# A one-hot selector made and refilled by halves in a fused four-layer graph kernel

## The reference, cut to what matters

```
nd = adj_d > 0                                    # neighbours that are kept
vals = jnp.where(nd[..., None], x[:, None, :, :], jnp.inf)
s = jnp.sort(vals, axis=2)                        # over the neighbours
nv = nd.sum(2)
for tau, w in zip((0.25, 0.5, 0.75), (0.25, 0.5, 0.25)):
    pos = tau * max(nv - 1, 0)
    lo, hi, frac = floor(pos), ceil(pos), pos - floor(pos)
    v_lo, v_hi = s at lo, s at hi                 # per node and feature
    agg = agg + w * (v_lo + frac * (v_hi - v_lo))
out = x + agg
y = (relu(out @ W1 + b1) @ W2 + b2) * mask
```

## Time and profile before

| | |
|---|---|
| median of three runs | 3531.01 us |
| profiled execution, device time | 3535.06 us |
| its span in the trace | 3533.3 us |
| busy: PE, DVE, ACT | 2577.4 us (73%), 2814.0 us (80%), 2151.4 us (61%) |
| share of the chain that ended last: PE, DVE, ACT, transfers | 47%, 23%, 19%, 3% |
| mean granted TensorE clock | 0.838 of full |
| rounds with units | 650 to 3200 us |

### The profile page before, as it was taken

One profiled execution on the slowest core, in us unless ns is written; L12 is line 12 of the kernel. 1 busy time (PEld: TensorE's weight loads), 2 busy tenths in 40 slices (PEclk: granted clock), 3 DMA queues, 4 the chain that ended last, 5 costly groups with the idle time before them and its releaser, 6 DMA issues.

```text
span 3533.3 us, 48449 instructions
## 1 busy us (share of the span) xinstructions
PE 2577.4 (73%) x17770; PEld 1184.8 (34%) x17770; DVE 2814.0 (80%) x5341; ACT 2151.4 (61%) x3176; POOL 13.7 (0%) x24
## 2 busy tenths in 40 slices
PE   0000114788888888888888888888888888986996
PEld 0000002333333333333333333333433343333665
DVE  7999989877878778787878787878778787745676
ACT  2112433677777777777777767777777777752232
POOL 0000000000000000000000000000000000000000
PEclk6555557899998989899999999998989999987777
DMA  2002000001010101001010101010100101010011
GB/s 63 0 0 60 6 0 21 10 19 22 19 29 9 33 10 31 12 27 19 19 20 19 19 20 31 9 29 11 33 9 29 19 19 20 2 26 24 25 36 36
DMA packets 157564, 74.67 MB, mean 21 GB/s; under 512 B 125192, under 2 KB 140698, under 8 KB 157082
## 3 DMA queue, kind: packets, MB, share of 16 engines
q1 hardware_dynamic: 153210, 70.68, 8.7%
q10 hardware_dynamic: 4128, 1.05, 0.2%
HBM read 42.27 MB, written 16.83 MB: 17 GB/s over the span
## 4 chain that ended last, share of the span: by engine, by line
PE 47%; DVE 23%; ACT 19%; issue 8%; DMA 3%; SPq 0%; DVEq 0%; ACTq 0%
PE rows L621 12%; PE ring L584 8%; PE found_bank L631 6%; ACT hot L1043 6%; PE bcast L597 5%; ACT below L1008 3%; DVE keys L1306 2%; DVE keys L1305 2%; PE bcast L702 2%; PE bcast L711 2%; ACT prod L1036 2%; PE bank L873 2%; DVE delta L1347 1%; DVE delta L1345 1%; DVE perm L1349 1%
## 5 line engine op out<-in xcount | busy, mean ns | idle before, releaser
L1043 ACT ACTIVATE hot<-bcast,consts 128x1024 bf16<-128x1024 f32 x744 | 831.9, 1118 | 235.8 <-PE bcast L597 235.1
L621 PE MATMUL rows<-hot,table 128*64 128x512 bf16 x4608 | 696.9, 411 | 0.0
L584 PE MATMUL ring<-member,neigh_t 128*128 128x512 bf16 x2048 | 524.2, 400 | 46.8 <-ACT words L1000 28.7
L1036 ACT ACTIVATE prod<-rows 128x512 f32<-128x512 f32 x600 | 361.6, 603 | 119.6 <-PE rows L621 119.4
L631 PE MATMUL found_bank<-prod,consts 128*64 128x512 f32 x1536 | 416.5, 621 | 0.0
L597 PE MATMUL bcast<-idx_t,consts 32*128 32x512 f16 x1488 | 306.9, 409 | 105.7 <-ACT hot L1043 103.4
L610 PE MATMUL rows<-fine_rows,consts 32*128 32x512 bf16 x768 | 310.5, 404 | 85.3 <-DVE prod L1455 52.8
L521 PE MATMUL ring<-identb,adj_b 128*128 128x128 bf16 x256 | 35.1, 266 | 387.2 <-ACT adj_b L928 376.0
L584 PEld LDWEIGHTS ring<-member,neigh_t 128*128 128x128 bf16 x2048 | 186.6, 102 | 370.1 <-issue 111.1
L621 PEld LDWEIGHTS rows<-hot,table 128*64 128x64 bf16 x4608 | 213.9, 113 | 271.2 <-issue 203.0
L1455 DVE TENSOR_SCALAR prod<-rows 128x512 f32<-128x512 f32 x168 | 115.6, 689 | 176.9 <-PE rows L621 171.6
(11 more groups left out here) (348 smaller groups left out, 4581.1 us busy)
## 6 DMA issues: line engine op xcount, KB each, us to landing
late<-in_adj_dram SPq DMA_DIRECT2D x16, 1024.0 KB, 5.3
fine_rows<-fine_t SPq DMA_DIRECT2D x512, 24.0 KB
adjt_d<-neigh_t SPq DMA_DIRECT2D x16, 512.0 KB, 2.7
adj_l<-adjt_d SPq DMA_DIRECT2D x16, 512.0 KB, 3.5
adj_s<-adjt_d SPq DMA_DIRECT2D x16, 512.0 KB, 3.4
parts_d<-parts SPq DMA_DIRECT2D x6, 512.0 KB, 5.2
table<-parts_d SPq DMA_DIRECT2D x192, 16.0 KB, 2.2
xt_d<-keys SPq DMA_DIRECT2D x2, 1024.0 KB, 9.2
```

Source lines behind the costliest of these rows:

```text
L584: ins = mm(ring[u % 2][:, :], kept_t[:, j, P * i:P * i + P], member[:, j, n // 2, 512 * (n % 2):512 * (n % 2) + 512], start=(j == 0), stop ...
L621: ins = mm(rows[u % 2][C * h:C * h + C, :], table[:, s, GROUPS * h + g8, :], hot[:, u % HOT, h, :], start=False, stop=(s == 2), skip_group ...
L1036: run(prod[:, u % DEEP, :], rows[u % 2][:, :], ACT.Relu).then_inc(S["prod_by_act"], 1)
L1043: run(hot[:, u % HOT].rearrange(flat), spread_bank(l, u)[0][:, 0:2, :].rearrange(flat), ACT.Relu, bias=eq_bias[:, :]).then_inc(S["hot_read ...
```

## The change

A unit's one-hot is made by two ACTIVATEs of 512 columns in place of one of 1024. Both semaphores between the two engines now count halves: each of the two broadcast matmuls signals `bc_ps` and waits for the matching half of the one-hot in front of it, and each ACTIVATE waits for its half and signals `hot_ready`. `lookup` still waits for both halves. The wait for a free `hot` buffer (`row_ps`) is in front of the first half.

```diff
@@ TensorE, spread(l, u) @@
                 to, behind = spread_bank(l, u)
-                if u >= behind:
-                    pe.wait_ge(S["hot_ready"], UNITS * l + u - behind + 1)
                 for h in range(2):
+                    if u >= behind:
+                        pe.wait_ge(S["hot_ready"], 2 * (UNITS * l + u - behind) + h + 1)
                     r = 32 * (2 * h + g8 // 4)
-                    ins = mm(to[:, h, :], sel_a[r:r + 32, at:at + P], idx_t[r:r + 32, k, :], start=True, stop=True, tile_position=(r, 0))
-                ins.then_inc(S["bc_ps"], 1)
+                    mm(to[:, h, :], sel_a[r:r + 32, at:at + P], idx_t[r:r + 32, k, :], start=True, stop=True, tile_position=(r, 0)).then_inc(S["bc_ps"], 1)
@@ TensorE, lookup(l, u) @@
-                pe.wait_ge(S["hot_ready"], UNITS * l + u + 1)
+                pe.wait_ge(S["hot_ready"], 2 * (UNITS * l + u) + 2)
@@ ScalarE, spread(l, u) @@
-                act.wait_ge(S["bc_ps"], UNITS * l + u + 1)
                 if u >= HOT:
                     act.wait_ge(S["row_ps"], UNITS * l + u - HOT + 1)
-                run(hot[:, u % HOT].rearrange(flat), spread_bank(l, u)[0][:, 0:2, :].rearrange(flat), ACT.Relu, bias=eq_bias[:, :]).then_inc(S["hot_ready"], 1)
+                for h in range(2):
+                    act.wait_ge(S["bc_ps"], 2 * (UNITS * l + u) + h + 1)
+                    run(hot[:, u % HOT, h], spread_bank(l, u)[0][:, h, :], ACT.Relu, bias=eq_bias[:, :]).then_inc(S["hot_ready"], 1)
```

## The result

The changed kernel takes 3570.65 us (median of four runs, 3570.16 to 3571.82) against 3531.3 (four runs, 3530.59 to 3532.71): a ratio of 1.0113, 95% interval 1.0097 to 1.0129. It is 39 us slower; the forecast was 3569.

The account below looks back on a forecast made before the run. The rounds were taken as mostly TensorE's own work, with ScalarE's one-hot 6% of the chain; 2.57 us a round over 15 rounds, taken as 38, on 3531 gave 3569 us. Range 3548 to 3593, 8 in 10 given the forecast.

Parts of the forecast that it names:

- The cost of two ACTIVATEs: ScalarE's one-hot: a second bias column and fixed part hold ScalarE 0.16 us more and end the one-hot 0.16 later.
- The early refill brings TensorE nothing: At TensorE's wait the second broadcast matmul, with `away` and `lookup` queued behind it, still needs the whole one-hot.
- What it brings ScalarE: Pauses of 0.12 and 0.49 us before the next `hot` go: at most 27 us of ScalarE's time.
- TensorE's waits on `hot` about 130 us: Profile after the change: TensorE's total wait on the one-hot grows from 103 us to about 130.
- A semaphore each way more at 0: Between TensorE and ScalarE: the added waits, where already met, are priced at 0.
- The 8 us that were to be kept for the upper end: If each met wait cost TensorE 10 ns, 768 units would make 8 us, kept for the range's upper end.
- Where 0.16 us lands: Per round: 11 TensorE waits, five second one-hots and the adjacency run, less one absorbed wait: 2.57 us, 38.6 in 15 rounds.
- The last graph adds nothing: In the last graph's units TensorE is busy 85.68 of 88 us and ScalarE 52, so longer one-hots add nothing.
- Cheap halves: Rival: a second ACTIVATE with the same bias column costs at most 0.48 us start to start; 5 us less, 3526; 6%.
- a winning refill: Rival: halves at 0.48 us let ScalarE's next unit start 0.12 to 0.49 us sooner; 32 us less, 3499; 4%.
- All of it lands: Rival: ScalarE becomes the bound in the rounds, 0.16 us at every unit; 115 us more, 3646; 7%.
- the cost is hidden: Rival: TensorE's waits just move and VectorE's chain ends the rounds; no change, 3531; 4%.

Follow-up runs that it names:

- experiment 4: Changed kernel with the bias column left out of both one-hot halves (computes something else): 3524.0 us, ratio 0.9977 to the kernel before.
- experiment 5: Kernel before, its single 1024-column one-hot ACTIVATE without the bias column (computes something else): 3498.1 us, ratio 0.9905.
- experiment 6: Kernel before, a second column operand (a scale) added to the single one-hot ACTIVATE, no splitting: 3563.0 us, ratio 1.0082.
- experiment 1: Changed kernel, but both broadcast matmuls wait until both one-hot halves are made, so nothing is refilled early: 3572.3 us, ratio 1.0114 to the kernel before.
- experiment 10: Kernel before, one ACTIVATE, with the broadcast put between the lookup's two halves at odd units of all graphs but the last: 3810.1 us, ratio 1.078.
- experiment 11: Changed kernel with broadcast matmuls and lookup halves alternating at odd units of all graphs but the last: 3793.5 us, ratio 1.0733 to the kernel before.
- experiment 2: Changed kernel with one ACTIVATE a unit again, signals and waits still by halves: 3540.9 us in twelve runs, repeated 3543.1 in ten; kernel before 3526 to 3538.
- experiment 9: Changed kernel with halves in the last graph's 48 units alone, one ACTIVATE elsewhere, all signals by halves: 3545.2 us, ratio 1.0041 to the kernel before.
- experiment 3: Changed kernel, both broadcast matmuls waiting for the whole one-hot, each with its own wait, the second always met: 3574.0 us.

## Why the prediction was right

The time came out within 2 us, in the range and on the forecast side, but not all of its steps held.

- *The cost of two ACTIVATEs.* Right, and this is the step that decided. Forecast about 690 ns a half, 1.27 us for the pair, 0.58 from start to start, 0.16 more on both counts (by its own numbers 1.16 - 1.01 is 0.15 on the second); measured 702, 1.27, 0.58 and 0.16 by the end, 0.13 to 0.14 by the start of what follows (1.14 or 1.15, not 1.16). ScalarE's busy time rose by 101 us and not 120: 744 times 0.13 to 0.14 is 97 to 104. Experiments 4, 5 and 6 show the column operand at 91, 89 and 92 ns. The Trainium skill (ScalarE: Activation LUTs, What ACT_TABLE_LOAD costs) has about 93 for each such operand, and these runs agree.
- *The early refill brings TensorE nothing.* Right in its effect: experiment 1 without it is 2 us from the change. That it is so because `away` and `lookup` are queued behind the second wait was argued from the order; the trace shows `away` going out with the second matmul, but experiments 10 and 11, meant to test it, don't.
- *What it brings ScalarE.* The pauses of 0.12 and 0.49 went, as said, and it didn't matter.
- *TensorE's waits on `hot` about 130 us.* In experiment 1 135; in the change itself the lone matmul hides them and the view says 70. I had not thought of how the view would count.
- *A semaphore each way more at 0.* Not right in general: signals and waits by halves cost 10 to 12 us in experiment 2, twice measured, and 15 in experiment 9; the met wait alone costs next to nothing in experiment 3. In the change's own 39 us it can't be told apart; if it is there in full, some 28 are left for the second ACTIVATE. The 8 us that were to be kept for the upper end are not in it: the clock alone gives 3591, and the range ends at 3593.
- *Where 0.16 us lands.* Right as a sum: 2.57 us a round forecast; 39 us over 15 rounds are 2.6, and the thirteen rounds of the traces are 2.2 apart. Not shown right as a list. By it even units should have cost 11 us more than odd ones, and both together 39. They cost the same, and 72 (50 against experiment 2). The slope is also steeper on the near side: experiment 6 gives 31 us for 0.09, the change 39 for 0.16. One term can be read from the waits: what VectorE's eviction absorbs was put at 0.16 us a round, and TensorE's wait for it in front of `away` fell from 52.8 us to 46.0, 0.45 a round. The terms had errors both ways and a handshake at nothing beside them, so that the sum came within 2 us of the measured time is partly luck.
- *The last graph adds nothing.* Right: TensorE is busy 83.7 of 88 us there, and experiment 9 adds 2 us over its like.
- *The rivals.* Cheap halves and a winning refill fall with 702 ns; experiment 4 shows that with halves at 611 ns the kernel would indeed have been a little faster than before, 7 us, near the 5 of the first rival, and nothing like the 32 of the second. "All of it lands" (3646) and "the cost is hidden" (3531) fall with the time.

## What to carry to other kernels

An ACTIVATE has a fixed part (a second one without a column held ScalarE 0.06 us more), and each operand that is a column in memory adds some 90 ns to it. Splitting one pays both again, 0.13 to 0.14 us here, and they show up where another engine waits for the *last* piece. A handshake by pieces gave next to nothing here. The reason that I give, that nothing behind the wait needs just the first piece, was argued from the order and not tested; still, look at what is queued there before you split. And when ScalarE's instruction is on the loop, look first for the operand that can go: here one bias column is worth 33 us, almost as much as the whole change lost, though no kernel that computes the same without it was built here.

## What was not expected of the hardware

- Two streams of matmuls with 64 output rows each (the two column halves of a lookup) run side by side when they stand in one piece: six took 0.84 us and three 0.83. Putting the broadcast between them cost some 19 us a round.
- TensorE's granted clock differs between rounds of equal work (0.91 and 0.94 of full, 168.2 and 166.2 us).
- Costs of parts do not add up: 37 and 35 us for two halves of a change that cost 39, at the same mean clock. Why is open.
- Signals and waits by halves, with all else as before, cost 10 to 12 us in the runs and nothing in the two executions that were profiled. What causes it is open.
